# Self attention stage: another order of work ahead of the projection, and operand copies made on the chip instead of loaded

## What is computed

```python
qkv = (x @ W_qkv).reshape(Bx, Nx, 3, H, D)
...
sim = (qg_n[None, None] * q_n).sum(-1).mean(-1)
sim = (sim - sim.min()) / (sim.max() - sim.min())
pos = sim > 0.9
logits = jnp.einsum('bqhd,bkhd->bhqk', q * scale, k)

def masked_attn(tok_mask):
    key_mask = jnp.concatenate([jnp.ones((Bx, REG), bool), tok_mask], axis=1)
    l = jnp.where(key_mask[:, None, None, :], logits, -jnp.inf)
    a = jax.nn.softmax(l, axis=-1)
    return jnp.einsum('bhqk,bkhd->bqhd', a, v)
x_pos = masked_attn(pos)
x_neg = masked_attn(~pos)
reg_out = (x_pos[:, :REG] + x_neg[:, :REG]) * 0.5
tok_out = jnp.where(pos[:, :, None, None], x_pos[:, REG:], x_neg[:, REG:])
out = jnp.concatenate([reg_out, tok_out], axis=1).reshape(Bx, Nx, Cx)
return out @ W_proj + b_proj
```

## Time and profile before

| | us |
|---|---|
| median of 3 runs | 2593.7 |
| runs shown | 2590.73, 2593.7, 2594.57 |
| profiled execution, device time | 2594.9 |
| profiled execution, span of the trace | 2593.1 |
| stage_self in the trace | from about 2252 to 2593 |
| mean granted TensorE clock | 0.973 |

### The profile page before, as it was taken

One profiled execution on the slowest core, in us unless ns is written; L12 is line 12 of the kernel. 1 busy time (PEld: TensorE's weight loads), 2 busy tenths in 40 slices (PEclk: granted clock), 3 DMA queues, 4 the chain that ended last, 5 costly groups with the idle time before them and its releaser, 6 DMA issues. The chain is left out here.

```text
span 2593.1 us, 47522 instructions
## 1 busy us (share of the span) xinstructions
PE 2474.5 (95%) x17128; PEld 2220.4 (86%) x17128; DVE 1824.8 (70%) x3030; ACT 1321.0 (51%) x2968; POOL 492.2 (19%) x412
## 2 busy tenths in 40 slices
PE   7899999999999999999999999999969999779988
PEld 7889999999999999999999999999858888667776
DVE  7467777777777777777777777777747666557766
ACT  3345555554555555555545555555534444445554
POOL 0311111111111111111111111111123333133332
PEclk9999999999999999999999999999969999879999
DMA  7645545555545555455555455554459999899993
GB/s 226 204 118 133 123 130 123 130 131 132 132 114 130 130 129 124 130 125 129 130 131 134 114 130 130 130 123 124 107 153 204 206 207 209 196 175 195 187 190 91
DMA packets 324313, 379.82 MB, mean 146 GB/s; under 512 B 125815, under 2 KB 231703, under 8 KB 324119
## 3 DMA queue, kind: packets, MB, share of 16 engines
q1 hardware_dynamic: 322414, 375.71, 60.9%
q10 hardware_dynamic: 1704, 1.43, 0.2%
HBM read 162.48 MB, written 72.57 MB: 91 GB/s over the span
## 5 line engine op out<-in xcount | busy, mean ns | idle before, releaser
L740 DVE TENSOR_TENSOR c_parted<-c_prob,c_parted 128x600 fp32r<-128x600 f32 x512 | 400.8, 783 | 363.2 <-ACT c_prob L686 363.2
L864 PE MATMUL c_mix<-c_parted,c_v 120*66 120x200 f32 (+1 forms) x3072 | 544.8, 270 | 0.7 <-DVE c_parted L740 0.6
L849 PEld LDWEIGHTS c_pair<-c_q_stack,c_k_stack 100*120 100x120 f32 (+1 forms) x3072 | 517.7, 186 | 10.7 <-issue 6.1
L849 PE MATMUL c_pair<-c_q_stack,c_k_stack 100*120 100x100 f32 (+1 forms) x3072 | 520.0, 227 | 6.2 <-DVE c_parted L740 4.8
L726 DVE TENSOR_REDUCE c_peak<-c_pair 100x1 f32<-100x724 f32 x512 | 457.0, 908 | 54.9 <-PE c_pair L811 39.6
L682 ACT ACTIVATE c_parted<-c_pair 128x600 fp32r<-128x600 f32 x512 | 344.5, 673 | 283.6 <-PE c_pair L849 283.4
L864 PEld LDWEIGHTS c_mix<-c_parted,c_v 120*66 120x66 f32 (+1 forms) x3072 | 418.3, 140 | 3.1 <-DVE c_parted L740 0.9
L686 ACT ACTIVATE c_prob<-c_pair 128x600 f32<-128x600 f32 x512 | 341.8, 667 | 0.0
L664 ACT ACTIVATE c_v<-c_work 120x512 fp32r<-120x512 f32 (+1 forms) x192 | 115.6, 602 | 442.3 <-PE c_work L91 442.3
L811 PE MATMUL c_pair<-c_k_stack,c_q_stack 96*100 96x362 f32 x1024 | 254.1, 329 | 0.0
L617 POOL TENSOR_TENSOR c_ct_lo<-e_stage,c_ct_hi 128x722 fp32r<-128x722 f32 x64 | 111.9, 1748 | 747.2 <-ACT c_ct_hi L650 747.2
(11 more groups left out here) (205 smaller groups left out, 5279.0 us busy)
## 6 DMA issues: line engine op xcount, KB each, us to landing
c_k_stack<-c_k_hi SPq DMA_DIRECT2D x1024, 90.2 KB, 2.1
e_stage<-in_ctx SPq DMA_DIRECT2D x32, 1444.0 KB, 6.4
c_k_stack<-c_k_lo SPq DMA_DIRECT2D x512, 90.2 KB, 2.1
c_q_stack<-q_parts SPq DMA_DIRECT2D x192, 100.0 KB, 2.4
mix_parts<-w_mixed SPq DMA_DIRECT2D x64, 200.0 KB, 3.2
r_parts<-mix_parts SPq DMA_DIRECT2D x22, 512.0 KB, 6.8
s_q_stack<-qk_parts SPq DMA_DIRECT2D x10, 800.0 KB
s_k_stack<-qk_parts SPq DMA_DIRECT2D x10, 800.0 KB
```

Source lines behind the costliest of these rows:

```text
L740: dve.tensor_tensor(p[:, :, 1, :], prob[i % 2][:], p[:, :, 0, :], ALU.subtract).then_inc(p_lo_done, 1)
L849: return pe.matmul(pair[i % 2][0:r, t // (CT // 2), col:col + S], k_stack[:, i, c_cols(t)], q_stack[:, i, :], start=True, stop=True)
L864: return pe.matmul(mix[g % 2][0:VW, at * 2 * S:(at + 1) * 2 * S], v[0:r, t, i, :], parted[i % PR][0:r, t, :, :].rearrange("p a s -> p (a s)"),
```

## The change

Three things, all in stage_self.

The projection's inputs. The reciprocal of group 3 (invert) moves from the body that uses it to the end of the body before. Folding the registers (fold_registers) moves ahead, between the shift of group 0 and turn_back of group 1; ot_hi is made by ScalarE (high_part), ahead of that body's exponentials; VectorE makes only ot_lo (split_mix), behind turn_back of group 1 and ahead of the shift of group 1.

The repeated thirds. From the third pair on, load_stacks starts two DMAs and not four; the repeated high parts are copied on the chip. q_stack's is copied by ScalarE, k_stack's by VectorE, each in four pieces of 32 partitions x 800 elements. Pieces 0 and 1 of a pair are copied in an odd body, 2 and 3 in the even body behind it: one between two exponentials (ScalarE) or ahead of turn_back of group 3 (VectorE), one at the end of the exponentials or behind the shift of group 3. For the third pair all four are in body 2. The last is in body 28.

POOL's register copies. They move from behind odd batches to behind even ones, so one body nearer to their use, and wait for the ScalarE pieces (q_third). The scores wait for q_third and k_third as well.

```diff
-A_PAIR_LOADS = 8
+WHOLE_LOADS, PAIR_LOADS = 8, 6
+WHOLE_PAIRS = 2
+def pair_landed(buf, before):
+    return 16 * (PAIR_LOADS * (before + 1) + (WHOLE_LOADS - PAIR_LOADS if buf < WHOLE_PAIRS else 0))
...
+def load_stacks(engine, qk_parts, q_stack, k_stack, first, landed, whole=True):
+    for stack, at, places in ((q_stack, SIDE, ((0, 0, 2), (2, 0, 1))), (k_stack, 0, ((1, 2, 2), (0, 2, 1)))):
+        for place, part, parts in places if whole else places[:1]:
...
+        def thirds_in(i, before, more):
+            ahead = (i + 3) // 2
+            if not more or (before < RING and ahead < WHOLE_PAIRS + (1 if i % 2 else 0)):
+                return 0, 0, ()
+            pieces = (0, 1) if i % 2 else (0, 1, 2, 3) if before < RING and ahead == WHOLE_PAIRS else (2, 3)
+            return ahead % STACKS, ahead // STACKS, pieces
...
+            def copies(buf, pairs_before, whole=False):
+                pool.wait_ge(pair_in[buf], pair_landed(buf, pairs_before))
+                if whole is not True:
+                    pool.wait_ge(q_third, HPT * (STACKS * pairs_before + buf - WHOLE_PAIRS + 1))
                 copy_registers(pool, q_stack[buf], unit_column, copies_done)
...
                     for j in range(HPT):
                         scale(u * RING + i, i % 2, j)
-                    if i % 2:
-                        copies((i + 3) // 2 % STACKS, u + (i + 3) // RING)
+                    if i % 2 == 0:
+                        copies((i + 2) // 2 % STACKS, u + (i + 2) // RING)
...
+            def high_part(b, odd):
+                rows = 0 if odd else SIDE
+                act.wait_ge(folded, 2 * b + 2)
+                act.activation(ot_hi[:], out_bank[odd][:, 0:KT * QR].rearrange("p (k q) -> p k q", k=KT)[:, :, rows:rows + S],
+                               ACT.Copy).then_inc(ot_hi_done, 1)
...
+                act.activation(q_stack[buf][2 * HD:3 * HD, heads, SIDE:SIDE + 2 * S],
+                               f32(q_stack[buf][0:HD, heads, SIDE:SIDE + 2 * S]), ACT.Copy).then_inc(q_third, 1)
...
+                dve.tensor_copy(k_stack[buf][0:HD, heads, 0:2 * S], f32(k_stack[buf][HD:2 * HD, heads, 0:2 * S])
+                                ).then_inc(k_third, 1)
...
+                    if not whole:
+                        pe.wait_ge(q_third, HPT * (STACKS * pairs_before + buf - WHOLE_PAIRS + 1))
+                        pe.wait_ge(k_third, HPT * (STACKS * pairs_before + buf - WHOLE_PAIRS + 1))
```

More of the change, by code:

```diff
@@ L925, in __init__ @@
         self.cleared, self.copies_done = m.sem("cleared"), m.sem("copies_done")
-def load_stacks(engine, qk_parts, q_stack, k_stack, first, landed):
-    for stack, at, places in ((q_stack, SIDE, ((0, 0, 2), (2, 0, 1))), (k_stack, 0, ((0, 2, 1), (1, 2, 2)))):
-        for place, part, parts in places:
+def load_stacks(engine, qk_parts, q_stack, k_stack, first, landed, whole=True):
+    for stack, at, places in ((q_stack, SIDE, ((0, 0, 2), (2, 0, 1))), (k_stack, 0, ((1, 2, 2), (0, 2, 1)))):
+        for place, part, parts in places if whole else places[:1]:
             src = qk_parts[part:part + parts].rearrange("a (d h) n -> (a d) h n", h=H)
@@ L1698, in _ @@
                     scale(b, b % 2, j)
-                if b % 2 and b + 3 < B:
-                    copies((b + 3) // 2 % STACKS, (b + 3) // RING)
+                if b % 2 == 0 and b + 2 < B:
+                    copies((b + 2) // 2 % STACKS, (b + 2) // RING, (b + 2) // 2 < WHOLE_PAIRS)
         @block.scalar
         def _(act):
+            def high_part(b, odd):
[3 more added lines that the diff above has]
+                               ACT.Copy).then_inc(ot_hi_done, 1)
             def exponentials(b, odd, j):
@@ L1711, in exponentials, with copy_third, body @@
                 last.then_inc(exp_done, 1)
-            def body(b, i, deep, pair, before, last):
+            def copy_third(buf, before, n):
+                act.wait_ge(pair_in[buf], pair_landed(buf, before))
+                heads = slice(n * HPT, (n + 1) * HPT)
+                act.activation(q_stack[buf][2 * HD:3 * HD, heads, SIDE:SIDE + 2 * S],
+                               f32(q_stack[buf][0:HD, heads, SIDE:SIDE + 2 * S]), ACT.Copy).then_inc(q_third, 1)
+            def body(b, i, deep, pair, before, last, u, more=True):
                 odd = i % 2
+                if before:
+                    high_part(b - 1, 1 - odd)
+                buf, turns, pieces = thirds_in(i, before, more)
+                half = len(pieces) // 2
                 if not last:
-                    for j in range(HPT):
-                        exponentials(b + 1, 1 - odd, j)
+                    exponentials(b + 1, 1 - odd, 0)
+                    exponentials(b + 1, 1 - odd, 1)
+                for n in pieces[:half]:
+                    copy_third(buf, u + turns, n)
+                if not last:
+                    exponentials(b + 1, 1 - odd, 2)
+                    exponentials(b + 1, 1 - odd, 3)
+                for n in pieces[half:]:
+                    copy_third(buf, u + turns, n)
                 if not before:
@@ L1724, in _ @@
             all_batches(act, body)
+            high_part(B - 1, 1)
         @block.vector
@@ L1767, in result, with copy_third, body @@
                                          ).then_inc(y_ready, 1)
-            def body(b, i, deep, pair, before, last):
+            def copy_third(buf, before, n):
+                dve.wait_ge(pair_in[buf], pair_landed(buf, before))
+                heads = slice(n * HPT, (n + 1) * HPT)
+                dve.tensor_copy(k_stack[buf][0:HD, heads, 0:2 * S], f32(k_stack[buf][HD:2 * HD, heads, 0:2 * S])
+                                ).then_inc(k_third, 1)
+            def body(b, i, deep, pair, before, last, u, more=True):
                 odd = i % 2
+                buf, turns, pieces = thirds_in(i, before, more)
+                half = len(pieces) // 2
                 turn_back(b, 0)
@@ L1773, in body @@
                     shift_of(b + 1, 0)
-                invert(b, odd, 3)
+                if before:
+                    fold_registers(b - 1, 1 - odd)
                 turn_back(b, 1)
+                if before:
+                    split_mix(b - 1, 1 - odd)
                 if not last:
                     shift_of(b + 1, 1)
-                if before:
-                    split_mix(b - 1, 1 - odd)
                 turn_back(b, 2)
@@ L1792, in body @@
                     invert(b + 1, 1 - odd, 2)
+                    invert(b + 1, 1 - odd, 3)
                 if not before:
@@ L1798, in _ @@
                 shift_of(0, j)
-            for j in range(HPT - 1):
+            for j in range(HPT):
                 invert(0, 0, j)
             all_batches(dve, body)
+            fold_registers(B - 1, 1)
             split_mix(B - 1, 1)
@@ L1853, in body @@
                 if not last:
-                    score(b + 1, at, 0, step + (i + 1) // RING)
+                    score(b + 1, at, 0, step + (i + 1) // RING, before < RING and (i + 1) // 2 < WHOLE_PAIRS)
                 if before:
```

40 lines of the change are left out of this document (19 added, 21 removed).

## The result

The changed kernel takes 2649.9 us (median of 4 runs, 2648.9 to 2651.0) against 2594.1 for the kernel before (median of 4 runs, the three shown above and one more): a ratio of 1.0217, interval 1.0205 to 1.0230. Every ratio in this document is to the kernel before, run beside the one in question; its interval is the 95% interval. The changed kernel is slower, inside the range of 2595 to 2654, and 26 us above the forecast of 2624.

The account below looks back on a forecast made before the run. PE was taken to set the pace. From the profiled 2594.9 us: start -10.2, batches 3 to 30 -2.2, last body's wait -0.7, together -13.1; clock falls +43; sum 2624.8, forecast 2624, range 2595 to 2654.

Parts of the forecast that it names:

- The projection's wait: Projection on PE: its 0.74 us wait for ot_lo goes, so a batch of PE work takes 8.5 us, not 9.25.
- The pieces: On-chip copies of 32 partitions x 800: about 0.86 us each on ScalarE, 0.6 on VectorE, the latter priced at nothing.
- Where the last piece ends: ScalarE's last piece in an even body ends at 9.3 us, so PE stands some 2.2 us in every pair, 14 times.
- The falls of the clock: PE's granted clock falls behind 10 of the 14 new idles, 4.3 us each: +43 us.
- The start: First batches: batch 2's transposes come at 2284.7, batch 3 begins at 2297.1 and not 2307.2: -10.2 us.
- The loads: DMA loads: a pair loses 800 KB; POOL's waits for tables go, and with them the stalls of 1.91 and 1.59 us.
- The end: Last body: its wait goes, -0.7 us.
- the clock holds: First rival: same schedule and 14 idles in PE, but no clock fall or hardly one: 2581 us, chance 0.15.
- every pair falls and long: Second rival: the clock falls in all 14 pairs at 4.9 us, 69 in place of 43: 2650 us, chance 0.1.
- the chain is not shorter: Third rival: ScalarE late to ot_hi, ot_lo misses the mix's end, 0.75 us returns in odd batches: +10, 2634 us, chance 0.08.
- VectorE and POOL get in each other's way: Fourth rival: VectorE's k pieces beside POOL's scaling cost each pair up to a scaling's length: some +5, 2629 us, chance 0.05.

## Why the prediction was right, and where its sizes were off

**The projection's wait.** Right. ot_hi starts 2.03 us behind the transposes (2.05 forecast), the projection follows the mix, and a body of PE work is 8.44 to 8.52 us (8.5 forecast).

**The pieces.** Right in length: 0.87 us on ScalarE (0.86), 0.565 on VectorE (0.57 to 1.0, 0.6 taken; from its rows the lower value comes to 0.54, and nothing hangs on it).

**Where the last piece ends.** Right in kind, 0.4 us short: 9.69 and not 9.3. The working let a middle piece push what follows by 0.8 us. The rows above show 1.40 us from the exponential ahead of it (2363.59) to the one behind it (2364.99) where two neighbours are 0.32 apart, so it pushes by 1.08: the copy starts at 2364.09, behind the end (2364.07) of the sum read of the last exponential, while the exponentials overlap a little with such reads (one starts at 2361.67, the read ahead of it ends at 2361.78). The last piece, too, starts only behind such a read. With the semaphores the idle is 2.7 to 2.9 and not 2.2. In the sum this is 146.5 us for 13 even bodies against 13 x 10.75 = 139.8: +7.

**The falls of the clock.** This is the term that was mis-sized most. It was set at 10 falls of 14 at 4.3 us, 43 us. There were 14, and the odd bodies took 175.3 us together against 14 x 8.45: 57 us, 4.07 each. Against the 14 x 8.5 of the sum it is 56, so +13. The price of one was right, and the run with filled idles gives it again (53 us, nearly all of it in 13 pairs). The number was guessed from three rows, 1.59, 1.91 and 2.46 us, all of which had been followed by a fall; the doubt that took 4 of 14 off named no row, though the trace of before holds one, the 1.71 us at its end that brought none. By the measured scale, no fall at 0.9 us, some at 1.4 to 1.7 and all from 2.0 on, an idle of 2.2 would have brought 14 as well.

**The start.** Right in direction: batch 2's transposes at 2286.58 (2284.7 forecast, 2293.79 before), batch 3's at 2299.48 (2297.1), so 2.4 us less gain than forecast. PE's wait ahead of batch 3 is 4.38 us, "nearly 4" in the forecast.

**The loads.** Right: no wait for tables after the start. And the stalls of 1.91 and 1.59 us went, as said.

**The end.** The last body's wait was to save 0.7 us. From the first transposes of batch 31 to the end of the trace it is 17.6 us and was 16.5, +1.8 against the sum: the last projection began at the lower level here, as shown above, and did not in the trace of before. The sum had no term for that.

The four differences, 7 + 13 + 2.4 + 1.8, are 24 of the 24.5 us between the 2624.8 of the sum and the profiled execution, 2649.3. All have one sign, so none made up for another.

**The rivals.** That the clock holds fell by 14 of 14. That every pair falls and long, 2650 at 14 x 4.9, gave the measured time, but by another sum: every pair fell, at 4.07 and not at 4.9, and the idle made up the rest. That the chain is not shorter fell. That VectorE and POOL get in each other's way did not show in the changed kernel: POOL idles while the last piece of the even body is copied, and where a scaling meets a piece it is the scaling that takes longer (1.23 us for 0.85, twice a pair), with no wait of PE for it inside a body. It was there all the same, and showed as soon as POOL's copies came earlier; there it cost 0.75 us a pair.

## What to carry over

A wait in the engine that sets the pace has two prices here, its own length and the clock's; fill it, or shorten it below what many of the kernel's own rows show to be harmless, before counting what it saves elsewhere. When work is added behind an in-order engine's loop, ask who needs the last of it and put that one into a gap further ahead: the same copies on the same engines, elsewhere in their order of work, were worth 92 us. And when one engine's work is moved earlier, look at what it now runs beside.

## What the runs showed of the hardware

**VectorE's copy inside SBUF and a POOL instruction shut each other out for most of their length.** In the kernel with ScalarE's pieces moved ahead, a scaling alone, a piece, and a scaling that starts 0.05 us behind that piece:
```profile
2299.26 0.85 POOL L1696 TENSOR_TENSOR s_prob<-s_prob,s_inv 106x400 f32<-106x400 f32 x1
...
2303.00 0.56 DVE L1817 CAST p_k_stack<-p_k_stack 32x800 fp32r<-32x800 f32 x1
...
2303.05 1.23 POOL L1696 TENSOR_TENSOR s_prob<-s_prob,s_inv 106x400 f32<-106x400 f32 x1 [2.94 <-DVE s_inv L1782]
```
Whichever comes second waits: the scaling takes 1.23 and not 0.85, and the piece behind a running scaling took 1.90 and not 0.56, up to the end of two scalings in a row. The first keeps its own time (0.56 for the piece, 1.67 for the two scalings), so this is no sharing that slows both. The second is longer by 0.38 of the 0.51 us that they overlap, and by 1.34 of 1.48, so all but some 0.13 us of the overlap is lost. Moving the piece away from POOL gave the 0.56 back and 8 us of the time. The Trainium skill (SBUF — State Buffer, "SBUF: two separate sides") describes an exclusive lock of the port pair that GpSimd shares with a VectorE operation in a two-port mode, held for a whole instruction by whichever starts first; the traces agree, but for those 0.13 us.

**The clock follows PE's own standing still, at lengths that look harmless.** With the gap filled the granted clock was 1.00 over 258 us, with the same work on every other engine. An idle of 2.0 us in a batch of 10.5 brought it down all 13 times, and the body behind it then took 2.9 to 4.7 us more, which is more than the idle. At 1.4 to 1.7 us equal idles in equal places went either way, so one trace in which such an idle did no harm does not show that it is harmless.
